# A query scale laid out by a one-element maximum, and a quantised attention stage with split chunk-bias products and a new order on four engines

## What is computed

```python
x = _layernorm(x + _L0_attn_ref(x, ...))
x = _layernorm(x + _L0_xattn_ref(x, ctx_2048, ...))   # 16 query heads of 128, 4 key heads, RMS norm of q and k
x = _layernorm(x + _L0_ffn_ref(x, ...))
x = _layernorm(x + _L1_attn_ref(x, ...))              # quantised attention, 32 heads of 8
x = _layernorm(x + _L1_xattn_ref(x, ctx_2048, ...))
x = _layernorm(x + _L1_ffn_ref(x, ...))

# in _L0_xattn_ref
q = rms_norm(q, q_norm_w)
probs = softmax(q @ k_full.T * scale + mask)
# in _L1_attn_ref, for the input and again for the context; chunks of 32 rows
ch_bias = (max over the chunk + min over the chunk) / 2
xz = xp - ch_bias
tmax, cmax = max |xz| of the chunk, of each of its columns
thr = tmax / 2 ** (7 .. 0);  idx = how many thr lie below cmax
scale = tmax / 2 ** (7 - idx) / 7
result = clip(round(xz / scale), -8, 7) * scale
y = result @ w_dq_t + ch_bias @ w_orig.T + b          # for q, k, v, and for the output
```

## Time and profile before

| what | value |
|---|---|
| median of 3 runs | 3069.39 us (3067.89 to 3073.41) |
| the profiled execution | 3069.82 us |
| its span in the trace | 3068.0 us |
| busy share of the span | PE 89%, DVE 65%, ACT 43%, POOL 41% |
| granted TensorE clock, mean | 0.949 |

### The profile page before, as it was taken

One profiled execution on the slowest core, in us unless ns is written; L12 is line 12 of the kernel. 1 busy time (PEld: TensorE's weight loads), 2 busy tenths in 40 slices (PEclk: granted clock), 3 DMA queues, 4 the chain that ended last, 5 costly groups with the idle time before them and its releaser, 6 DMA issues. The chain is left out here.

```text
span 3068.0 us, 64499 instructions
## 1 busy us (share of the span) xinstructions
PE 2738.8 (89%) x23444; PEld 2348.4 (77%) x23444; DVE 1997.8 (65%) x4030; ACT 1321.8 (43%) x3154; POOL 1261.2 (41%) x1605
## 2 busy tenths in 40 slices
PE   6999999995899999999999789996999999699993
PEld 6888888884788888888888678885777777477772
DVE  5555555554788888888888654443776776466667
ACT  2222222222666666666666432221333333266666
POOL 3111111112566666666666401112444444334444
PEclk9999999997999999999999999996888888799998
DMA  3000000002000000000000010000000000000001
GB/s 135 7 7 7 4 7 7 7 0 93 4 5 3 5 3 5 3 5 3 5 3 5 7 64 0 0 0 29 11 8 7 10 7 3 18 29 27 27 11 56
DMA packets 42503, 49.10 MB, mean 16 GB/s; under 512 B 4032, under 2 KB 33600, under 8 KB 41920
## 3 DMA queue, kind: packets, MB, share of 16 engines
q1 hardware_dynamic: 42432, 48.16, 4.8%
HBM read 35.56 MB, written 4.19 MB: 13 GB/s over the span
## 5 line engine op out<-in xcount | busy, mean ns | idle before, releaser
L1078 POOL TENSOR_TENSOR b_rows<-b_rows,b_swapped 128x512 f32<-128x512 f32 x160 | 204.0, 1283 | 133.0 <-DVE b_swapped L865 133.0
L1019 ACT ACTIVATE b_probs<-bank,b_shift,b_q_scale 128x128 f32<-128x128 f32 x512 | 227.8, 458 | 70.9 <-DVE b_shift L896 70.7
L46 PE MATMUL bank<-a_xT,a_wq 128*128 128x256 f32 x512 | 151.2, 295 | 49.6 <-DVE a_xT L371 49.6
L505 POOL TENSOR_TENSOR a_probs<-a_probs,a_rs 128x512 f32<-128x512 f32 x64 | 66.8, 1043 | 305.6 <-DVE a_rs L404 298.3
L1125 POOL TENSOR_TENSOR b_probs<-b_probs,b_rs 128x512 f32<-128x512 f32 x128 | 133.1, 1040 | 110.9 <-DVE b_rs L916 107.4
L1088 POOL TENSOR_TENSOR b_rms<-b_rms,sh_minus_half 128x8 f32<-128x8 f32 (+1 forms) x128 | 169.6, 1325 | 10.7
L124 POOL TENSOR_SCALAR sh_rstd<-sh_meanvar 128x2 f32<-128x2 f32 (+1 forms) x80 | 17.8, 222 | 376.1 <-DVE sh_meanvar L116 264.0
L873 DVE TENSOR_REDUCE b_ss<-b_squares 128x4 f32<-128x512 f32 x192 | 125.2, 680 | 60.7 <-ACT b_squares L994 60.7
L46 PE MATMUL bank<-b_wo,b_oT 128*128 128x256 f32 x512 | 150.4, 294 | 1.4 <-DVE b_oT L839 1.4
L46 PE MATMUL bank<-a_wo,a_oT 128*128 128x256 f32 x512 | 146.6, 286 | 0.0
L47 PE MATMUL bank<-a_xT,a_wq 128*128 128x256 f32 x512 | 145.8, 285 | 0.0
(11 more groups left out here) (350 smaller groups left out, 9147.8 us busy)
## 6 DMA issues: line engine op xcount, KB each, us to landing
a_xT_in<-in_xT SPq DMA_DIRECT2D x16, 256.0 KB, 2.7
sh_x<-in_x SPq DMA_DIRECT2D x1, 4096.0 KB, 25.0
b_ctx_in<-in_ctxT SPq DMA_DIRECT2D x32, 128.0 KB, 2.0
d_x_in<-sh_x SPq DMA_DIRECT2D x16, 256.0 KB, 2.3
e_x_in<-sh_x SPq DMA_DIRECT2D x16, 256.0 KB, 2.4
e_cT<-in_ctxT SPq DMA_DIRECT2D x32, 128.0 KB, 2.6
out<-sh_x SPq DMA_DIRECT2D x16, 256.0 KB, 2.1
a_qT<-in_L_attn_Wq SPq DMA_DIRECT2D x1, 2048.0 KB, 8.6
```

The source lines that it names most:

```text
L46: pe.matmul(out, left[0], right[0], start=start, stop=False)
L1019: op = act.activation(probs[:, g % 2, keys], bS[:, keys], ACT.Exp, bias=shift[:, g % 2, a:a + 1], scale=q_scale[:, g, a // 2, a % 2:a % 2 ...
L1078: pool.tensor_tensor(rows[:, unit, :], rows[:, unit, :], swapped[:, half, :], ALU.add).then_inc(added[unit], 1)
```

## The change

In `spread_q` each of the four copies of 64x8 elements becomes a maximum (`tensor_reduce`) over an added axis of length one; the values are the same. In `spread_x` each product with 128x128 weights becomes two with 128x64 weights, one for each half of the result's partitions, alternating; the semaphore is still raised behind the last. And the lists of PE, DVE, ACT and POOL in the quantised stage are written anew. The values that are computed, the tiles, the semaphores and the functions called are the same, but for which unit a bank or a buffer is waited for with (`scores(mid, 1, 1)` waits for shift 2 instead of 3, the two `take_att` for other last units, as `weigh` has another order). Where a call stands at the other end of the list with a neighbouring unit (`project_v(new, 0)` at the end becomes `project_v(mid, 0)` at the head), it is the same step of the same unit on the other side of the turn's border. In the list of each engine of the quantised stage, from PE's on, the lines without a sign stay.

```diff
   for h in range(2):
       for b in range(2):
-          op = dve.tensor_copy(q_scale[h * S:(h + 1) * S, :, :, b],
-                               rms[b * S:(b + 1) * S, Q:NU, :].rearrange("p g (a h) -> p g a h", h=2)[:, :, :, h])
+          op = dve.tensor_reduce(q_scale[h * S:(h + 1) * S, :, :, b],
+                                 rms[b * S:(b + 1) * S, Q:NU, :].rearrange("p g (a h) -> p g a h", h=2)[:, :, :, h].unsqueeze(3),
+                                 AX.X, ALU.max)
   op.then_inc(q_scale_ready, 1)
...
           at = YB.start + (m * C + o) * M
           for c in range(C):
-              op = pe.matmul(bX[1][:, at:at + M], w[:, m, c, o * 128:(o + 1) * 128], qx.bias[:, c * M:(c + 1) * M],
-                             start=(c == 0), stop=(c == C - 1))
+              for side in range(2):
+                  op = pe.matmul(bX[1][side * 64:(side + 1) * 64, at:at + M],
+                                 w[:, m, c, o * 128 + side * 64:o * 128 + (side + 1) * 64], qx.bias[:, c * M:(c + 1) * M],
+                                 start=(c == 0), stop=(c == C - 1))
   op.then_inc(qx.top_spread, 1)
...
+  project_v(mid, 0)
+  turn_x(new, oldest)
   scores(mid, 0, 0, 5, True)
-  weigh(old, 7)
-  turn_x(new, oldest)
+  scores(mid, 0, 1, 7, True)
+  weigh(old, 4)
+  turn_probs(old, 7, 6, False)
   project_v(mid, 1)
   weigh(old, 6)
-  scores(mid, 0, 1, 7, True)
+  weigh(old, 7)
+  turn_probs(mid, 0, 7, True)
   scores(mid, 1, 0, 1, False)
-  turn_probs(mid, 0, 7, True)
   turn_att(old, mid)
+  turn_probs(mid, 1, 0, False)
+  scores(mid, 1, 1, 2, False)
   weigh(mid, 0)
-  turn_probs(mid, 1, 0, False)
-  scores(mid, 1, 1, 3, False)
   turn_probs(mid, 2, 1, False)
   weigh(mid, 1)
-  weigh(mid, 2)
   turn_cmax(new, qx, bX[1], qc, old, v_taken[1])
   turn_probs(mid, 3, 2, False)
   spread_x(new)
+  weigh(mid, 3)
   turn_probs(mid, 4, 3, False)
   turn_cmax(old, qc, bX[0], qx, new, res_ready)
-  weigh(mid, 3)
+  weigh(mid, 2)
   turn_probs(mid, 5, 4, False)
...
   project_k(new, old, 1)
   project_q(new, 0)
-  weigh(mid, 4)
   project_q(new, 1)
-  turn_probs(mid, 7, 6, False)
   project_out(old, new, 0)
   project_out(old, new, 1)
-  project_v(new, 0)
...
+  moments(oldest)
+  lowest(new, qx, bX[0])
+  maximum(mid, 0)
+  highest(new, qx, bX[0])
+  shift(mid, 0)
+  maximum(mid, 3)
+  maximum(mid, 1)
   shift(mid, 1)
-  lowest(new, qx, bX[0])
-  highest(new, qx, bX[0])
-  take_att(old, 1, 6)
   maximum(mid, 2)
-  maximum(mid, 3)
+  shift(mid, 3)
+  take_att(old, 1, 7)
   shift(mid, 2)
-  widest(new, qx)
-  shift(mid, 3)
+  maximum(mid, 5)
   lowest(old, qc, bX[1])
   highest(old, qc, bX[1])
-  centre(new, qx, bX[0])
+  widest(new, qx)
   maximum(mid, 4)
   centre(old, qc, bX[1])
   shift(mid, 4)
   find_top(new, qx, bX[1])
-  maximum(mid, 5)
+  centre(new, qx, bX[0])
   widest(old, qc)
   shift(mid, 5)
   thresholds(new, qx, bX[1])
+  maximum(mid, 7)
   maximum(mid, 6)
-  maximum(mid, 7)
-  shift(mid, 6)
-  count(new, qx)
   add_bias(new)
   find_top(old, qc, bX[0])
-  take_att(mid, 0, 3)
+  count(new, qx)
+  shift(mid, 6)
+  take_att(mid, 0, 2)
   invert(new, qx)
   thresholds(old, qc, bX[0])
   divide(new, qx)
   restore(new, qx, v_ready)
   count(old, qc)
-  shift(mid, 7)
   invert(old, qc)
   divide(old, qc)
   restore(old, qc, y_ready)
   take_k(new)
+  shift(mid, 7)
   take_q(new)
   residual(old)
-  moments(old)
-  maximum(new, 0)
-  maximum(new, 1)
-  shift(new, 0)
...
+  exponent(old, 6)
+  exponent(old, 7)
+  take_pT(old, 6)
+  exponent(mid, 0)
+  take_pT(old, 7)
+  take_v(mid, 0)
+  take_v(mid, 1)
+  exponent(mid, 1)
+  take_pT(mid, 0)
+  take_pT(mid, 1)
   exponent(mid, 2)
-  take_pT(mid, 1)
   exponent(mid, 3)
   take_pT(mid, 2)
+  take_pT(mid, 3)
   exponent(mid, 4)
-  take_pT(mid, 3)
   exponent(mid, 5)
   take_pT(mid, 4)
-  exponent(mid, 6)
   take_pT(mid, 5)
-  take_pT(mid, 6)
-  exponent(mid, 7)
-  take_pT(mid, 7)
-  take_v(new, 0)
-  exponent(new, 0)
-  exponent(new, 1)
-  take_v(new, 1)
-  take_pT(new, 0)
...
+  compare(oldest, qc)
   find_scale(oldest, qc)
-  spread_bias(mid, qx, v_ready)
+  spread_bias(oldest, qc, y_ready)
   spread_k(mid)
+  add_out_bias(old)
+  find_bias(new, qx)
+  find_spans(new, qx)
   if oldest is not None:
       normalise(pool, sh, oldest.n, 2, meanvar_ready, norm_step, norm_done)
-  find_bias(new, qx)
-  find_spans(new, qx)
   find_bias(old, qc)
+  spread_bias(new, qx, v_ready)
   find_spans(old, qc)
   compare(new, qx)
   find_scale(new, qx)
-  add_out_bias(old)
-  spread_bias(old, qc, y_ready)
-  compare(old, qc)
```

## The result

The changed kernel takes 2969.71 us (median of four runs, 2964.81 to 2972.07) against 3068.82 us before, measured beside it: a ratio of 0.9668, 95% interval 0.9657 to 0.9680, some 99 us. The forecast was 2991.8 with a range of 2972 to 3018: the direction and the two stages were right, the gain was 22 us larger than forecast, and the time lies just under the range. The profiled execution took 2967.99 us, its span 2966.0.

The account below looks back on a forecast made before the run. PE was taken to bound both touched stages, by waits and half clock. 3069.8 less 38.4 (cross-attention) and 39.6 (quantised stage) gave 2991.8 us; forecast's own range 2980 to 3003, 8 in 10 for 2972 to 3018.

Parts of the forecast that it names:

- The saving is the wait, not the 2.15: Cross-attention: 2.15 us less on DVE removes PE's wait before `scores` (L725); only that wait counts as saving.
- 39.4 less one at the ends, 38.4 us: Cross-attention: PE's 39.4 us in 32 waits before L725 go, less one at the ends, saving 38.4 us.
- what might be late next: Cross-attention: the addition for `turn_unit(mid, Q + 3)` behind `rope` moves forward with the same 1.8 us; no saving summed.
- Maxima not held: `spread_q` in cross-attention: four one-element maxima run unheld beside POOL, 0.17 us each, 0.7 in all.
- some 0.5 us: Cross-attention: time to spare before `scores` (L725) once its wait is gone, some 0.5 us.
- Chunk products: `spread_x`, quantised stage: 32 half-tile records take 1.05 us instead of 1.81, 0.76 us less.
- Rival (d): `spread_x`: a half tile costs a whole one's time, 3.6 us instead of 1.05; total 3030; chance 0.05.
- the estimate of 0.4 us more: `spread_x`: by the skill's overhead rule, 16 extra records would cost 0.4 us more instead of 0.76 less.
- The walk: Quantised stage, new order stepped through at full clock: 29.4 us a turn, PE's own work 26.9, four waits.
- The clock: Quantised stage: clock still falls in most turns, late, returning within k or q; half clock 2 to 7 us a turn.
- I take 1.3: Quantised stage: dense work at half clock adds 1.3 us a turn, making 30.7; bounds 29.4 and 32.1.
- The first two turns: Start of quantised stage: earlier `turn_x`, shorter `spread_x` at half clock and one period save 2.6 + 2.5 us.

## Why the prediction was short of the gain

**Cross-attention: mechanism right, term too small.** "The saving is the wait, not the 2.15" held: the copies' time fell by 2.2 us a turn and 1.6 came out. The step that failed is "39.4 less one at the ends, 38.4 us": measured 51.5. The idle time in a row starts at the modelled end of the record before. In the earlier trace rows the idle before L725 is 1.24, but issues tell more. The kernel before has, in PE's timeline:

```profile
1114.95 0.60 PE L714 MATMUL bank<-sh_ident,b_rows 128*128 128x128 f32 x4
1116.79 0.27 PE L725 MATMUL bank<-b_causal,b_ident 128*128 128x256 bf16 x1 [1.24 <-ACT b_probs L1019]
...
1117.96 0.66 PE L714 MATMUL bank<-sh_ident,b_rows 128*128 128x128 f32 x4
```

From the first L714 to L725 it is 1.84 us, after 0.44: 1.40 gained where 1.24 was shown. From L725 to the second L714 it is 1.17, after 1.00: 0.17 more. That is a second wait. The prediction named it as what might be late next ("the addition for `turn_unit(mid, Q + 3)`, behind `rope` on DVE, which moves forward") and had no term for it in the sum. The kernel before has it in its timeline:

```profile
1116.63 1.27 POOL L1078 TENSOR_TENSOR b_rows<-b_rows,b_swapped 128x512 f32<-128x512 f32 x1 [3.89 <-DVE b_swapped L865]
...
1117.96 0.42 PEld L714 LDWEIGHTS bank<-sh_ident,b_rows 128*128 128x128 f32 x4 [0.20 <-POOL b_rows L1078]
```

The addition ends at 1116.63 + 1.27 = 1117.90, just before PE's L714; it stands behind `rope` and came earlier with it. Together 1.57 us in each of 32 turns, 50 us. With three reductions behind the wait both came back, 1.0 and 0.17 us.

**Maxima not held**: right, 0.67 us for four with 0.7 forecast, under POOL's additions, and the shift held instead (0.36 us instead of 0.16 in the turn shown, until POOL's additions ended). Margin "some 0.5 us": 0.7, confirmed by one reduction that is free and three, 1.86 us, that cost 1.2 a turn behind the wait.

**Chunk products**: 1.05 forecast, 0.95 measured. Rival (d) is out: twice the records took half the time. The Trainium skill (TensorEngine Tiling (Array Packing), Instruction Overhead) warns against taking a tiling factor from a dimension that is already small. That warning was misapplied in the prediction and does not bear on this edit: the 8 columns stayed 8, and what was halved is the 128 of the weights; the estimate of 0.4 us more, drawn from that section, did not come true.

**The walk**: 29.4 at full clock forecast, 29.82 measured. Waits forecast 0.4, 1.0, 0.75 and 0.35, measured 0.41 (before `turn_probs 1`), 0.98, 0.34 and 0.85. The sum of 2.6 against 2.5 is right; the last two changed sizes. The rest is PE's own work, 27.2 us for 26.9.

**The clock**: "I take 1.3" was the second failed size; it cost 30.35 - 29.82 = 0.53. The clock fell late, as forecast, or not at all, in five turns of thirteen, and 3.4 us a turn on average is within the 2 to 7 given. A turn with 3.4 us of it was 0.2 to 0.6 us longer, one with 10.2 was 2.1; the stretches cover waits too. That its fall is rarer than assumed is owed to the two edits together: with the order alone every turn still had 6.8 or 10.2 us of it. Walk and clock together: 30.35 for 30.7, 4.6 us over thirteen turns. That this is so near is in part luck: the clock was priced 0.8 too high and the walk 0.4 too low.

**The first two turns**: 5.1 forecast, 12.2 measured, the third. The sum took the old turns less one edit each. But in the second the clock had stood at 0.75 and stays at 1.00 now, a step that the forecast had only for the steady turns. With the order alone they take 22.20 + 27.59, with the half tiles alone 22.23 + 32.25, and only both bring 46.6. This part varies by the execution: the trace with one reduction behind the wait, the same code in this stage, has 21.58 + 27.66, with 6.8 us of half clock in the second. For the drain a loss of 1.2 was forecast and 1.8 measured (the last transpose of `turn_x` to the end of the stage: 82.9 before, 84.7 after).

So 51.5 - 38.4 = 13, 7 and 4.6, less 0.6 of the drain, make 24 us, for 2991.8 - 2968.0 = 24 missing in the profiled execution. The first three err the same way. The range was the forecast's range for the clock alone: no bound was set on what one wait of 1.23 us in 32 turns is worth, and by the trace of before that was the largest term.

## What to carry to other kernels

A small copy or two-input operation of VectorE within SBUF that stands between GpSimd's long ones can take 1.2 us for 8 elements, eight times its own length; look at the maximum of its duration, not the median, and try a reduction of one input. When a wait of TensorE is costed, take it from issue to issue in the two timelines (next start less last start, less the pitch of such records), and ask what else stands behind the instruction that moves earlier. Before work is put on an engine's path, ask on which side of its wait it stands: 1.9 us ahead of one cost 6 us in all, behind it 35.

## What the hardware showed that was not expected

- In these traces DVE's operation form decides whether 8 elements take 0.16 or up to 1.24 us beside POOL; `tensor_tensor` of one tile with itself is held like the copy (690 ns median for 156).
- A product with 128x64 weights and 8 columns is issued every 30 ns, with 128x128 weights every 113: a half costs about a quarter, not a half. The halves alternate between the two sides of the result; how much is owed to that, and how much to their size, no run here separates.
- The granted clock reacts to what fills PE's waits: three products of 256 columns a turn took it from 0.94 to 0.99 over thirteen turns. The time hardly followed (30.35 to 30.09 us a turn, within what this stage varies by): the changed kernel's half-clock stretches cost it only 0.5 us a turn, and the one stretch that was left cost 3.4 us.
